# A four-block sequence model in one kernel: weight loads regrouped in the front, dummy matmuls fewer, the last chunk in halves

## Time and profile before

| | us |
|---|---|
| median of 3 runs (lowest, highest) | 677.53 (676.58, 678.08) |
| the profiled execution | 677.15 |
| its span, first to last instruction | 675.0 |
| PE busy in the span | 621.2 |
| DVE busy | 422.7 |
| ACT busy | 388.7 |
| mean granted TensorE clock | 0.969 of full |

### The profile page before, as it was taken

The page is one execution under the profiler, slowest core; times in us unless marked ns, Lnnn a source line. Parts: engine busy times, 40 slices in busy tenths (PEclk is TensorE's granted clock), DMA queues, the critical chain, the costliest instruction groups (busy, mean ns, idle before and its releaser), DMA issues.

```text
span 675.0 us, 9501 instructions
## 1 busy us (share of the span) xinstructions
PE 621.2 (92%) x3490; PEld 416.0 (62%) x3490; DVE 422.7 (63%) x851; ACT 388.7 (58%) x743; POOL 92.2 (14%) x121
## 2 busy tenths in 40 slices
PE   4677698899999999999999999999999999999896
PEld 2313477644458878744468878654588787454586
DVE  1622896498637475788366665986374757981544
ACT  1401777246785467467884476477855584668610
POOL 1004230122000000640000003610000006300000
PEclk9955999899999999999999999999999999999999
DMA  8999630512000002431000006220000005210000
GB/s 288 386 368 299 192 126 32 119 25 50 1 1 1 2 0 59 92 74 32 1 1 1 0 7 137 62 50 2 1 1 0 1 19 100 66 39 2 1 0 33
DMA packets 34975, 45.08 MB, mean 67 GB/s; under 512 B 4848, under 2 KB 28016, under 8 KB 34800
## 3 DMA queue, kind: packets, MB, share of 16 engines
q1 hardware_dynamic: 30096, 32.04, 16.4%
q0 software_dynamic: 3488, 10.49, 5.7%
q10 hardware_dynamic: 1344, 1.94, 1.4%
HBM read 28.32 MB, written 3.15 MB: 47 GB/s over the span
## 4 chain that ended last, share of the span: by engine, by line
PE 68%; DVE 12%; DMA 8%; ACT 7%; issue 2%; SPq 1%; ACTq 0%; POOL 0%; POOLq 0%
PE psum L1430 21%; PE psum L1707 9%; PE psum L1826 8%; PE psum L1696 8%; PE psum L1652 8%; DVE mx L1258 7%; DMA early_pieces<-in_hyp_w 6%; PE psum L1597 2%; PE psum L1738 2%; PE psum L1533 2%; PE psum L1542 1%; ACT arena L767 1%; PE psum L1719 1%; ACT act L686 1%; ACT arena L686 1%
## 5 line engine op out<-in xcount | busy, mean ns | idle before, releaser
L1258 DVE TENSOR_REDUCE mx<-psum 128x1 f32<-128x512 f32 x256 | 159.1, 681 | 29.0 <-PE psum L1652 29.0
L911 ACT ACTIVATE arena<-psum 128x512 f32<-128x512 f32 x256 | 140.6, 602 | 57.0 <-PE psum L1696 55.0
L1652 PE MATMUL psum<-kst,qst 96*128 96x512 f32 x192 | 79.3, 437 | 1.7 <-DVE mx L1258 0.8
L1696 PE MATMUL psum<-qst,kst 98*128 98x512 f32 x192 | 77.2, 422 | 1.8 <-ACT arena L911 1.8
L1430 PE MATMUL psum<-upw_hi,kst 128*128 128x512 f32 x256 | 72.5, 405 | 3.1 <-DVE arena L1201 2.6
L1707 PE MATMUL psum<-arena,vals 128*17 128x512 f32 x512 | 67.4, 598 | 1.4 <-ACT arena L911 1.0
L1826 PE MATMUL psum<-act,ghw_hi 128*128 128x512 f32 (+1 forms) x216 | 63.2, 365 | 1.0 <-DVE act L1038 0.2
L501 POOL DMA_DIRECT2D kst<-split x36 | 18.1, 509 | 328.6 <-DMA kst<-split 288.2
L1652 PEld LDWEIGHTS psum<-kst,qst 96*128 96x128 f32 x192 | 36.2, 188 | 39.1 <-DVE mx L1258 30.4
L1430 PEld LDWEIGHTS psum<-upw_hi,kst 128*128 128x128 f32 x256 | 47.2, 192 | 13.4 <-DVE arena L1201 3.1
L1696 PEld LDWEIGHTS psum<-qst,kst 98*128 98x128 f32 x192 | 35.4, 189 | 20.7 <-ACT arena L911 17.1
(11 more groups left out here) (219 smaller groups left out, 1163.4 us busy)
## 6 DMA issues: line engine op xcount, KB each, us to landing
early_pieces<-in_hyp_w SPq DMA_DIRECT2D x17, 512.0 KB, 8.5
arena<-in_hyp_w SPq DMA_DIRECT2D x15, 512.0 KB, 8.7
kst<-split POOLq DMA_DIRECT2D x36, 128.0 KB, 3.9
qst<-split SPq DMA_DIRECT2D x60, 64.0 KB, 3.6
arena<-in_x SPq DMA_DIRECT2D x4, 512.0 KB, 3.4
arena<-in_up_w POOLq DMA_DIRECT2D x8, 256.0 KB, 4.5
arena<-in_gh_w POOLq DMA_DIRECT2D x8, 256.0 KB, 4.2
out_x<-arena SPq DMA_DIRECT2D x8, 256.0 KB, 2.1
```

The source lines that it names most:

```text
L911: s.activation(probs[:, kb % 2, i, :], bank[3 + n % RING], ACT.Exp).then_inc(a_p, 1)
L1258: v.reduce_max(mx[:, g % 2, col:col + 1], bank[u % RING], AX.X).then_inc(d_max, 1)
L1652: pe.matmul(bank[u % RING], qst[g % 3][0:KROWS, i, P * t:P * t + P], keys_of(g)[0:KROWS, i // 2, :], start=True, stop=True).then_inc(e_max, 1)
L1696: pe.matmul(bank[3 + k % RING], keys_of(g)[0:SROWS, i // 2, P * kb:P * kb + P], qst[g % 3][0:SROWS, i, :], start=True, stop=True).then_inc ...
```

## The change

- **Up loads.** POOL waits for ACT's first eviction of the down product before it issues loads 4 to 7. Loads 8 to 11 no longer wait for the last store. The late stages now lie in the tile `act`, and POOL clears that tile for queries only when all low parts are done.
- **ACT's front.** `front_bottleneck` first, then weights 0 to 3, a dummy root (its table), weights 4 and 5, `front_h2`, weights 6 and 7, the store, the rest.
- **DVE's front.** The down product's low part and `first_weights(1)` first, weights 0 and 1, `front_x2`, `front_h2`, then six low parts (weights 2 to 7) and the reciprocal. `query_key_weights` goes to n = 1 of the row loop, late rounds 0 to 3 to n = 2 to 5, rounds 4 and 5 behind the queries and keys (on ACT behind its two query DMAs). The three additions of `other_weights` go behind the two low parts of the attention's input and behind the low parts of queries and keys.
- **Queries.** SP issues the low part of the even heads in every batch, as the first of its query DMAs.
- **Dummies.** Front 14 for 16, the last four behind a wait for DVE; batch 0: 12 for 14, with no wait for the values, and none for 4 before the scores (in other banks); the three single ones of the other batches and their leading two go; last batch 2 for 6.
- **Last chunk.** In the last batch chunk 7 goes through PE, ACT and DVE in two halves of 256 rows (the second in banks 4 and 5), and each half of the output is signalled by itself.

```diff
-def gated_bank(f, last):
-    return 2 * ((f if last else f + NOW) % 2)
+def gated_bank(f, last, h=0):
+    return 4 if h == 1 and last and f == HT - 1 else 2 * ((f if last else f + NOW) % 2)
+def gated_parts(f, last):
+    return HALVES if last and f == HT - 1 else (slice(0, L),)
...
-        stage = [cut(col, 512) for col in (3072, 3584, 8192, 8704)]
+        stage = [cut(col, 512) for col in (8192, 8704, 3072, 3584)]
-        late_stage = [cut(col, 512) for col in (2048, 2560, 6144, 6656)]
+        late_stage = [late_pieces[:, 512 * k:512 * k + 512] for k in range(STAGES)]
... SP, stack_q
-                for e in range(1 if g == 0 else 0, 2):
+                for e in range(2):
                     for k, part in enumerate((0, 1, 0)):
+                        if g == 0 and e == 0 and part == 0:
+                            continue
... POOL
             pool.wait_ge(e_piece, 2 * NPIECE)
+            pool.wait_ge(a_dn, 1)
             for n in range(STAGES, UP):
                 load_stage(n)
...
-            for i in range(2):
-                pool.wait_ge(hyp_stored[i], 16 * 4 * NPIECE // SLOT // 2)
             pool.wait_ge(hyp_moved, 16 * 2)
             for i in range(2):
                 pool.wait_ge(hyp_straight[i], MOVED)
-            for n in range(UP, NSPLIT):
+            for n in range(UP, UP + STAGES):
+                load_stage(n)
+            for i in range(2):
+                pool.wait_ge(hyp_stored[i], 16 * 4 * NPIECE // SLOT // 2)
+            for n in range(UP + STAGES, NSPLIT):
                 load_stage(n)
...
                     pool.wait_ge(e_maxT, b * NG + 1)
+                    pool.wait_ge(d_wlo, NSPLIT)
... ACT, batch
-                        if first:
-                            late_weights(n)
+                        if first and n in (2, 3, 4, 5):
+                            late_weights(n - 2)
...
-                even_queries(((0, 0), (2, 0)), a_qk)
+                even_queries()
+                if first:
+                    late_weights(4)
+                    late_weights(5)
                 for h in range(2):
-                    if h == 1:
-                        even_queries(((1, 1),), d_qk)
... ACT, front
-            for k in range(2):
+            front_bottleneck(0, first_dn)
+            for k in range(4):
                 weights(k)
-            front_bottleneck(0, first_dn)
-            for k in range(2, UP):
+            s.activation(warm[:, :], eps6, ACT.Sqrt)
+            for k in range(4, 6):
+                weights(k)
+            front_h2(0)
+            for k in range(6, UP):
                 weights(k)
             store(NPIECE // SLOT - 1)
-            front_h2(0)
... DVE, batch
-                        if first:
-                            late_weights(n)
+                        if first and n == 1:
+                            query_key_weights()
+                        if first and n in (2, 3, 4, 5):
+                            late_weights(n - 2)
...
                 lo_parts(b * 2, a_h3, inp[0], inp[1], d_h3, slice(0, HALF))
+                if first:
+                    other_weights(1)
                 lo_parts(b * 2 + 1, a_h3, inp[0], inp[1], d_h3, slice(HALF, L))
+                if first:
+                    other_weights(2)
...
+                if first:
+                    other_weights(3)
+                    late_weights(4)
+                    late_weights(5)
... DVE, front
-            for k in range(2):
-                weights(k)
             front_bottleneck(0, first_dn)
             first_weights(1)
-            for k in range(2, 4):
+            for k in range(2):
                 weights(k)
             front_x2(0, 0, x2T)
             front_x2(0, 1, x2T)
             front_h2(0)
-            for k in range(4, UP):
+            for k in range(2, UP):
                 weights(k)
-            query_key_weights()
             front_rms(0)
-            other_weights()
... DVE, output
-                if h == 0:
-                    v.wait_ge(e_out, f * NOW if signal is d_part else (B - 1) * NOW + HT)
+                if signal is not d_part:
+                    v.wait_ge(e_out, (B - 1) * NOW + HT + h)
+                elif h == 0:
+                    v.wait_ge(e_out, f * NOW)
... PE, batch
-                pe.wait_ge(a_v, b * 2 + 2)
-                keep_clock(bank[6], 14 if first else 2)
+                if first:
+                    keep_clock(bank[1], 12)
+                else:
+                    pe.wait_ge(a_v, b * 2 + 2)
                 for u in range(FIRST_MAX):
                     max_tile(u)
                     if first:
-                        keep_clock(bank[6], 1)
+                        keep_clock(bank[3], 1)
...
-                    if u >= G * T + 2 and not first:
-                        keep_clock(bank[4], 1)
-                if first:
-                    keep_clock(bank[6], 4)
...
-                    keep_clock(bank[0], 6)
+                    keep_clock(bank[0], 2)
... PE, swiglu_out (ACT's and DVE's loops over f get the same halves)
-                    pe.wait_ge(d_hh, b * (3 * NOW) + 3 * f + 3)
+                    parts = len(gated_parts(f, last))
                     for t in range(T):
+                        if t % (T // parts) == 0:
+                            pe.wait_ge(d_hh, b * (3 * NOW) + 3 * f + 3 + 3 * (t * parts // T))
...
-                    ins.then_inc(e_out, 1)
+                        if (t + 1) % (T // parts) == 0:
+                            ins.then_inc(e_out, 1)
... PE, front
-            for _ in range(16):
+            for k in range(14):
+                if k == 10:
+                    pe.wait_ge(d_dn, 1)
```

More of the change, by code:

```diff
@@ L820, in batch, with even_queries @@
                                  ).then_inc(a_qk, 1)
-                def even_queries(parts, ready):
-                    s.wait_ge(ready, b * 4 + 4)
-                    for k, part in parts:
-                        src = split[0:DH, 4 * part:4 * part + 2, :]
+                def even_queries():
+                    s.wait_ge(a_qk, b * 4 + 4)
+                    for k in (0, 2):
+                        src = split[0:DH, 0:2, :]
                         dst = qst[0][32 * k:32 * k + DH, 0::2, :]
@@ L937, in batch @@
                 for f in range(HT if last else NOW):
-                    s.wait_ge(e_gh, b * NOW + f + 1)
                     if f >= 2:
                         s.wait_ge(d_hh, b * (3 * NOW) + 3 * (f - 2) + 1)
-                    s.activation(sg[:, f % 2, :], bank[gated_bank(f, last)], ACT.Silu).then_inc(a_silu, 1)
+                    for h, cols in enumerate(gated_parts(f, last)):
+                        s.wait_ge(e_gh, b * NOW + f + 1 + h)
+                        s.activation(sg[:, f % 2, cols], bank[gated_bank(f, last, h)][:, cols], ACT.Silu
+                                     ).then_inc(a_silu, 1)
                     if not last:
@@ L1818, in batch, with gated @@
                 pe.wait_ge(a_h4, b * 8 + 2)
[L1820 removed]
+                def gated(f, k, cols, part, h):
                     col = k * HID + P * f
@@ L1847, in batch @@
                         pe.wait_ge(d_hh, b * (3 * NOW) + 3 * (f - 2) + 1)
-                    for h in range(2) if f == 0 else (None,):
-                        if h == 1:
+                    for h, cols in enumerate(HALVES if f == 0 else gated_parts(f, last)):
+                        if f == 0 and h == 1:
                             pe.wait_ge(a_h4, b * 8 + 6)
-                        cols = slice(0, L) if h is None else slice(HALF * h, HALF * h + HALF)
                         for part in range(2) if f == 0 else (None,):
```

36 lines of the change are left out of this document (19 added, 17 removed).

## The result

| | before | after |
|---|---|---|
| median of 4 runs each, us (lowest, highest) | 677.47 (676.58, 678.08) | 672.31 (671.75, 672.95) |
| span of the profiled execution | 675.0 | 670.1 |
| mean granted TensorE clock | 0.969 | 0.964 |

The ratio is 0.9925 with a 95% interval of 0.9908 to 0.9942. The change is worth 5.2 us where 9.7 were forecast; 672.31 lies 4.5 us over the forecast and 0.3 outside its range. The sign was right, the size was not.

The account below looks back on a forecast made before the run. The chain was taken as mostly PE (68%), with holes before the row loop's first DVE product and the first row maximum. 3.2 + 3.9 + 1.9 + 0.7 = 9.7 off 677.53 gave 667.8 us; range 664.0 to 672.0.

Parts of the forecast that it names:

- the term of 3.2: Front: DVE's first product of the row loop comes at 80.0 in place of 83.15, a gain of 3.2 us.
- The moves: Front: with up loads 4 to 7 held back, DVE's bottleneck addition starts near 67.6 instead of 70.12, 2.5 us sooner.
- The hidden table load: Front, ACT: the root's 1.28 us table load moves ahead of weights 4 and leaves the path from h2 to Gelu.
- The first attention: Start of batch 0's attention: first row maximum at 125.5 against 129.38, gain 3.9 us; bounds 1.4 and 4.2.
- The rival of the late queries: Attention starts: tiles wait for SP's low part; gain 1.4 in the first batch, 0.15 each in others; 671.7 us; chance 0.12.
- The rival of the row loop: First batch's row loop: about 1.5 us lost to PE's half clock comes on top; 666.3 us or little less; chance 0.15.
- Batches 1 to 3: Removed dummies there gain 0.6 us per batch, 1.9 us for three; bounds 0 and 2.3.
- The end: Last batch: halving the last hidden chunk lets DVE start at 669.1, not 669.80, gain 0.7 us; bounds 0 and 0.8.
- nothing, if the clock stays: Last batch: dropping four of six dummies gains nothing, since PE waits for DVE's norm until 632.9 either way.
- the clock rival: Front, first and a later attention, last batch: fewer dummies let the clock fall, 1.5 us lost each; all four 673.8; chance 0.05.
- The slower rival: Row loop: ACT holds a Gelu behind a late load, each microsecond over 6.3 costing two; 678.9 us; chance 0.03.
- little front: Front rival: moves still land at 70, gain 2.1, or later loads take 7.3 us, gain 0.9, 670.1; chance 0.12.

Follow-up runs that it names:

- e1: Kernel after, with POOL's two query memsets moved ahead of its wait for the down product: 667.44 us, ratio 0.9869.
- e4: As e1 (early memsets), with six dummy matmuls instead of two ahead of the last batch's SwiGLU: 667.49 us, ratio 0.9872.
- e9: As e1 (early memsets), with the five dummy matmuls put back in batches 1 to 3: 668.65 us, ratio 0.9889.
- e12: As e4 (early memsets, six dummies), with chunk 7 of the last batch whole again instead of halved: 668.27 us, ratio 0.9887.
- e7: As e1 (early memsets), without POOL's wait for the down product before up loads 4 to 7: 667.26 us, ratio 0.9841.
- e8: As e1 (early memsets), without the dummy root ahead of weights 4, so its table loads where the root is: 668.78 us, ratio 0.9868.
- e6: Kernel before, with only the attention's part changed: SP issues the even queries' low part, 12 dummies without the values' wait, none before the scores: 673.35 us, ratio 0.9932.
- e2: Kernel after, memsets left late, DVE's cast of the second bottleneck weight replaced by a rounding addition with two SBUF inputs: 667.57 us, ratio 0.9876.
- e5: Kernel before, with POOL's query memsets directly behind its waits for the small moves, ahead of the wait for the last store: 678.02 us, ratio 1.0008.
- e3: Kernel before, with POOL's query memsets behind its waits for the small moves and the last store: 680.5 us, ratio 1.0059.
- e11: As e7 (early memsets, no down-product wait), plus six dummies in the last batch and the rounding addition for the cast: 667.15 us, ratio 0.987.

## Why the prediction was wrong, and where it was right

**The step that failed** is in the front: "queued behind that wait are these loads, the two query memsets and all later weights". The memsets were named and put on no clock. A line from the same view would have done it: POOL's two memsets last 3.6 us from 64.81 in the kernel before; behind the wait and four issues of 2.1 they run from 68.6 to 72.2, and DVE's cast, moved by the same change from 70.58 to about 68.1, falls into that time. In the kernel before it came after them. So the overlap of the cast with the memsets is the step that failed: the term of 3.2 measured -0.45, and with the memsets out of the way 3.3 to 4.5 (e1, e4, e9, e12). That e1's time (667.44) is nearly the forecast of 667.8 is in part luck: its gain of 9.05 against the forecast's 9.7 has a larger front and a smaller end.

The rule that would have raised the question is in the Trainium skill, "SBUF — State Buffer", in the section on two separate sides: a vector instruction in a two-port mode and a GpSimd instruction use one shared pair of ports, and whichever starts first holds it for its whole length, while the other waits. The runs agree in the main: the same cast took 0.29 us alone, 1.55 beside one memset, 4.09 beside two. They show who waited for whom; that a port is the reason is the page's account, and no run tests it. Not all fits: in the kernel after the profile puts the start of the cast (68.26) ahead of the memsets' (68.63), and yet the cast waited for both.

**The rest of the front was right in kind and too small.** The moves: 67.6 forecast, 67.81 measured, with the reason (loads behind moves) borne out by the traces under e7. The hidden table load: 1.28 counted, 1.28 by e8. The loads of weights 4 and 5 landed sooner than the 4.7 us taken from the earlier trace rows: issued at 65.93 in e1, copied from 69.97. So h2 started at 71.03 and not at 71.8, and from there to the Gelu it took 6.86 us and not 7.5: the first product came at 78.64 and not at 80.0. With the memsets away the term was 0.1 to 1.3 too small.

**The first attention**: 3.9 forecast, 3.82 measured, and 3.4 for its own part in e6. That the number is so near is luck, since two errors cancelled. The forecast had all three even queries there by 124.7, with 2.9 us for ACT's DMAs and 2.5 for SP's. SP's took 2.8. ACT's second, now beside it, took 3.67, and 3.57 to 3.69 in the nine other traces that have this order. But everything lay nearer to the first product than in the kernel before: PE's last product of the values 37.68 us behind it and not 38.18, since the new row loop is shorter. The rival of the late queries was right on the wait (1.05 us, ended by a query DMA), but it expected SP's low part to be the late one, and 2.5 us of loss where there was none. The rival of the row loop gave 0.5 of its 1.5 us, and by e6 not by the clock that it named.

**Batches 1 to 3**: 1.9 forecast, 1.14 in the kernel after, 1.45 in the mean of eight traces, all of it from the dummies (e9). The term was sized too high: the forecast had 0.6 us a batch of the dummies on the chain and did not see what is late next: the maxima rows' DMA, 1.83 us, in one batch of the kernel after 2.38.

**The end**: 0.7 forecast, 0.26 measured. The halves gave 0.8 (e12), at the upper bound given. What failed here is "nothing, if the clock stays": the clock rival had a hole of 1.5 us as its bound and took 1.70 as survived. The hole here was 1.31 us. So that a hole was survived at one place said nothing for another. The warning of the Trainium skill that the forecast named ("TensorE: Matmul & The Clock Gate", HAM oscillation) stands: idle gaps can throttle the engine again, and at this place four executions of six bear it out and two don't.

**The slower rival** did not come: no instruction of ACT waits for a load inside the row loop, and the loop got 0.5 us shorter.

**The range** was narrower than its own terms. Its lower end adds 1.5, 0.3 and 0.4 to the gain, which makes 665.6 and not 664.0. Its upper end is given as late queries with little front, but by the rivals' own figures those two together make 672.8 (front 2.1) to 674.0 (front 0.9), not 672.0.

## What to carry to other kernels

When a wait is put into a queue, write down the new time of every instruction behind it, also of those that the change is not about, and lay these times beside what the other engines do then: POOL can hold DVE up without sharing a tile or a semaphore with it. An instruction that takes ten times its usual length without an idle time before it is such a case, and moving one of the two is the test. Dummies can be worth their place in one stage (six ahead of the last batch, and the clock stayed) and cost time in another (fifteen in batches 1 to 3, 1.45 us), so price them one place at a time.

## What the runs showed that I had not expected

- A DVE cast of 128x256 from SBUF to SBUF: 0.29 us alone, 1.55 and 4.09 beside POOL's memsets of 1.83 us each. Subtractions with two inputs in SBUF kept their length beside the same memsets (two of 128x512 in 1.28 us in e2, 1.29 in the kernel before).
- The cast can get in between two memsets (e5) or not (the kernel after). In e5 the second memset's record is then 1.95 us long and not 1.83. What decides it stays open.
- The front's clock can fall without a held cast. PE's six matmuls of the up product took 2.92 or 2.93 us in all four traces where PE had stood idle 3.46 to 4.38 us before them (the kernel after, e3, e5, e6), and 1.64 to 1.67 where the hole was 0.19 to 1.77. e3 and e6 have the front of the kernel before up to there, whose own trace has the hole of 1.77. What differs is the clock: it was at 1.00 from 64 us, where the kernel before had 0.50 till 66, and in e3 the 16 dummies that fill the hole took 3.80 us in place of 4.59.
- The same hole of 1.30 to 1.31 us before the last batch's turns, with the same two dummies ahead of it, was followed by a granted clock of 0.50 to 0.61 in the kernel after, e1, e2 and e7, and by 1.00 in e8 and e9. With six dummies (hole 0.40) it stayed at 1.00 in all of e4, e11 and e12. So the fall is a matter of the execution, not of the hole's length alone; what decides it was not found.
- The small DMA of the maxima rows took 1.82 to 2.38 us ahead of a batch's first scores, and 3.0 to 3.6 at a later place of batch 1 (318.08 in the kernel after).
- A 64 KB query DMA of ACT took 2.7 us in the kernel before and 3.57 to 3.69 in all ten traces in which SP issues a third one just ahead of it (0.06 us in the kernel after).
